# A gated cross-attention block on one core: the value table's product in 16-bit halves, its pieces staged elsewhere, and the last gate's small steps on GpSimd

## The chip, the cores and the metric

The kernel runs on one core of one Trainium2 chip. The metric is device microseconds from start to end of the program, the median of several runs; lower is better. Beside these runs there is one profiled execution, from which all rows below come. The engines are TensorE (PE; PEld is its weight load), VectorE (DVE), ScalarE (ACT), GpSimd (POOL) and SyncE (SP), which here only issues DMAs.

## The reference

Eight batches of 224 rows by 2048 columns pass through cross-attention against 750 context rows and then through a gated feed-forward block with a table of 512 slots:

```
x = x + tanh(g_xattn) * attention(layernorm(x), ctx, ctx, mask)     # 32 heads, 8 KV heads, 64 wide
h = layernorm(x)
query = h @ Wq.T                                                    # 64 wide
router = (query @ Wr.T) @ (aux_keys @ Wr.T).T / sqrt(48) + log_rel  # 512 slots, top 8 kept
w = softmax(query . aux_keys[top] / 8 + log_rel[top])
aux = (w @ aux_values[top]) @ Wvd.T @ Wvu.T                         # 512 slots -> 2048 -> 128 -> 2048
u = clip(0.5 * log1p(var) / mean(log1p(var)) + 2.5 * sigmoid(gelu(h @ Wu1.T + bu1) @ Wu2.T + bu2), 0, 5)
gate = sigmoid(gate_w1 * clip((u - 0.5) / 1.5, 0, 1) + gate_bias), 0 where < 0.05
x = x + tanh(g_ffn) * (h + gate * aux)
```

## The kernel before

There are two phases. The attention phase (to about 885 us) goes through 64 groups of seven units each; its order is written out by hand, and each engine has its own list of steps joined by semaphores. The feed-forward phase works on 14 tiles of 128 rows. The last part of the attention and the first steps of the feed-forward phase overlap.

fp32 accuracy is had from 16-bit products: a number is split in a high half (either its upper 16 bits, read in place by `high`, or a rounded copy) and a low half, the difference, and a product is summed as high x high + high x low + low x high. The attention, the wide product with Wu1 (`sum_wide`) and the last product with Wvu (`aux_part`) are done so. Two products of the feed-forward phase are fp32 instead:

- `sum_v2` (L1031 to L1038) builds the table v2 = aux_values @ Wvd.T, 512 slots by 128, once, in PSUM bank 6. The 2048 inner columns come as 8 pieces (`load_piece`: `av_stage`, 512 KB, and `wvd_stage`, 128 KB, in one of three staging slots); each piece has 8 matmuls of 128x128. Pieces 3 to 7 are loaded as slots come free (`v2_piece`). The staging slots lie in the arena behind the tiles x2b[0] to x2b[2], over xn, k_raw and k_lo of the attention. ScalarE copies v2 out (L813).
- `sum_z(t)` (L1079 to L1083) multiplies v2 with the turned weights `w_t` of tile t: four matmuls of 128x128. Ahead of it `turn_w` transposes the softmax weights and `copy_w` (ScalarE, L789) copies them out of PSUM; behind it `round_z` (L793) and `split_z` (L1409) split the result.

SyncE's queue at the border of the phases (L478 to L496) is, in this order: Wvu; a wait for the last scores; b1, w2, rel; pieces 0 to 2; the spill of the last batch's 96 lower rows, twelve DMAs, after a wait for x_added; a wait until these have landed; pieces 3 to 7; the six reloads x2b[0] to x2b[5], from the fourth on after the end of sum_v2; the stores.

TensorE's list between the phases (L1099 to L1121): turn_h, sum_query(0,0), the key products, sum_wide and sum_query of tile 0, turn_h(1,0), v2 pieces 0 and 1, quarter 2 of tile 0, turn_h(1,1), pieces 2 and 3, quarter 3 of tile 0, turn_h(1,2), pieces 4 and 5, turn_h(1,3), route(0), pieces 6 and 7. Then iterations t = 1 to 13: sum_query(t, 0 to 2), sum_wide(t, 0), turn_w(t-1), sum_query(t, 3), ..., route(t), sum_z(t-1), the rest of sum_wide, with turn_h(t+1, j) between, and from t = 8 on `aux_part` of finished tiles. `turn_h(t, j)` transposes a quarter of a normalised tile, ScalarE rounds it (`round_h`, L699), VectorE takes the low half (`split_h`, L1293).

VectorE's list of an iteration holds, among others, split_h and stage_h, `select` (the top 8 of the router row, L1362 to L1376), `dot` (L1357), `join_query` (L1388), which route(t) waits for, statistics of later tiles in iterations 1 to 5 (L1260), and `finish` (L1405), the last addition to a quarter of a tile. ScalarE does the exp of the weights (`weigh`), the GELU, and the copies.

GpSimd, after the attention, scales the keys and takes their low half (L621, L623), computes the roots of the tiles' variances (`root2`), low halves of Wvu (L633), and then the gates of the tiles in six chains of small operations (`GATES`, L659 to L671, each with a wait on the one before). The last tile's gate is computed by VectorE (L1501 to L1512) with ScalarE's exps (L842, L845) between, in the tail, where the 12 last `aux_part` of tiles 11, 12 and 13 are finished and stored.

## Time and profile before

| | |
|---|---|
| median of 3 runs (lowest, highest) | 1178.43 us (1178.39, 1180.54) |
| profiled execution: its own time | 1179.06 us |
| profiled execution: span, first to last instruction | 1177.3 us |
| granted TensorE clock, mean of the span | 0.999 |
| busy: PE, DVE, ACT, POOL | 97%, 80%, 78%, 76% |
| attention; overlap and v2; tiles 1 to 13; tail | to 885; 885 to 916; 916 to 1165; to 1177 us |

Shares of the whole span average over two phases with different lists. TensorE's matmuls are pipelined, so their modelled ends overlap the next start; the spacing of starts is the price of one. The table by stage and the timelines are therefore read beside the shares. The chain that ended last runs for 73% over TensorE and for 20% over GpSimd; the latter is in the attention.

### The profile page before, as it was taken

What the parts mean: (1) busy time and instruction counts of PE and PEld (TensorE: products, weight loads), DVE (VectorE), ACT (ScalarE), POOL (GpSimd) and SP (SyncE); (2) the same over time, 40 slices, a digit from 0 to 9 for tenths busy, and PEclk for the clock granted to TensorE, in tenths of its full rate; (3) what the DMA queues carried; (4) which work ended last, traced back from release to release, by engine and by line L of the source; (5) the groups of instructions that cost most, each with busy time, mean ns of one, the idle gap of its engine ahead of it and who ended that gap; (6) DMA issues with size and microseconds to landing.
All of it is one profiled execution on the core that took longest, in us unless ns stands there. A gap on an engine that the chain in (4) does not pass through costs nothing.

```text
span 1177.3 us, 35064 instructions
## 1 busy us (share of the span) xinstructions
PE 1139.6 (97%) x14385; PEld 913.8 (78%) x14642; DVE 944.6 (80%) x2255; ACT 916.7 (78%) x1226; POOL 889.9 (76%) x804
## 2 busy tenths in 40 slices
PE   5999999999999999999999999999999999999997
PEld 3888888888888888888888888888887665555554
DVE  5988888888888888888888888888874899676765
ACT  5899898888998898998899988999881444555544
POOL 6899999999999999999999999999991110404222
PEclk9999999999999999999999999999999999999999
DMA  9421231132114212311321131121225500011224
GB/s 336 148 69 48 57 116 45 52 83 97 42 42 116 70 48 57 115 49 48 86 93 42 46 78 49 42 58 51 62 87 182 209 2 1 1 68 77 107 99 152
DMA packets 60735, 95.09 MB, mean 81 GB/s; under 512 B 35233, under 2 KB 44449, under 8 KB 56482
## 3 DMA queue, kind: packets, MB, share of 16 engines
q1 hardware_dynamic: 59858, 91.79, 25.4%
q8 instruction: 118, 1.93, 0.7%
q10 hardware_dynamic: 720, 1.05, 0.3%
q14 instruction: 39, 0.32, 0.1%
HBM read 71.75 MB, written 20.97 MB: 79 GB/s over the span
## 4 chain that ended last, share of the span: by engine, by line
PE 73%; POOL 20%; DMA 2%; issue 2%; DVE 2%; SPq 1%; ACT 0%; DVEq 0%; POOLq 0%
POOL arena L590 14%; PE psum L985 12%; PE psum L932 12%; PE psum L909 11%; PE psum L939 6%; PE psum L920 6%; PE psum L962 5%; PE psum L956 5%; PE psum L957 5%; PE psum L1066 3%; POOL arena L557 2%; PE psum L972 2%; PE psum L999 2%; PE psum L887 2%; POOL arena L610 1%
## 5 line engine op out<-in xcount | busy, mean ns | idle before, releaser
L590 POOL TENSOR_TENSOR arena<-arena 128x768 bf16<-128x768 f32 x448 | 651.8, 1470 | 40.2 <-ACT arena L719 37.6
L1303 DVE CUSTOM_DVE_ANT_0 arena<-psum,arena 128x750 f32<-128x750 f32 x448 | 420.5, 939 | 127.4 <-PE psum L920 121.9
L719 ACT ACTIVATE arena<-psum 128x768 f32<-128x768 f32 x448 | 362.2, 809 | 89.4 <-PE psum L939 89.3
L723 ACT ACTIVATE arena<-arena,neg_max 128x750 f32<-128x750 f32 x448 | 410.9, 917 | 3.8 <-DVE neg_max L1303 3.7
L932 PE MATMUL psum<-ident,arena 128*128 128x128 f32 x1792 | 268.8, 273 | 0.0
L956 PEld LDWEIGHTS psum<-arena 128*128 128x128 bf16 (+1 forms) x2688 | 194.7, 98 | 57.6
L909 PE MATMUL psum<-arena 128*128 128x512 bf16 x674 | 222.5, 384 | 14.9 <-DVE arena L1200 0.8
L957 PE MATMUL psum<-arena 128*128 128x64 bf16 (+1 forms) x2688 | 222.2, 193 | 0.0
L956 PE MATMUL psum<-arena 128*128 128x65 bf16 (+1 forms) x2688 | 221.9, 194 | 0.0
L957 PEld LDWEIGHTS psum<-arena 128*128 128x128 bf16 (+1 forms) x2688 | 178.5, 98 | 53.2
L932 PEld LDWEIGHTS psum<-ident,arena 128*128 128x128 f32 x1792 | 206.7, 140 | 4.3
L939 PE MATMUL psum<-ident,arena 128*128 128x128 f32 x896 | 171.5, 273 | 0.2 <-ACT arena L719 0.2
L920 PE MATMUL psum<-arena 128*128 128x238 bf16 x896 | 167.5, 268 | 0.9 <-DVE neg_max L1303 0.9
L962 PE MATMUL psum<-arena 128*128 128x65 bf16 (+1 forms) x2688 | 160.1, 194 | 1.3 <-POOL arena L590 1.3
L985 PE MATMUL psum<-arena 128*128 128x512 bf16 x648 | 156.8, 384 | 1.5
L985 PEld LDWEIGHTS psum<-arena 128*128 128x128 bf16 x672 | 63.6, 96 | 75.0 <-issue 0.8
L962 PEld LDWEIGHTS psum<-arena 128*128 128x128 bf16 (+1 forms) x2688 | 114.9, 98 | 1.9 <-POOL arena L590 1.9
L939 PEld LDWEIGHTS psum<-ident,arena 128*128 128x128 f32 x896 | 112.2, 141 | 0.5 <-ACT arena L719 0.4
L699 ACT ACTIVATE arena<-psum 128x512 bf16<-128x512 f32 x56 | 33.3, 597 | 96.2 <-PE psum L972 96.2
L1246 DVE SCALAR_TENSOR_TENSOR arena<-psum,r_den,arena 128x64 f32<-128x64 f32 x448 | 97.5, 278 | 2.3
L557 POOL TENSOR_TENSOR arena<-arena 128x750 bf16<-128x750 f32 x64 | 92.1, 1439 | 1.8 <-DMA arena<-in_k_t 1.8
L909 PEld LDWEIGHTS psum<-arena 128*128 128x128 bf16 x896 | 87.8, 98 | 6.1 <-issue 0.8
(161 smaller groups left out, 1267.1 us busy)
## 6 DMA issues: line engine op xcount, KB each, us to landing
arena<-in_k_t SPq DMA_DIRECT2D x128, 187.5 KB, 3.2
arena<-in_v_rows SPq DMA_DIRECT2D x64, 192.0 KB, 2.5
out<-arena SPq DMA_DIRECT2D x12, 1024.0 KB, 3.9
arena<-in_x_top SPq DMA_DIRECT2D x8, 1024.0 KB, 5.3
arena<-in_x_rest SPq DMA_DIRECT2D x8, 768.0 KB, 4.5
spill<-arena SPq DMA_DIRECT2D x96, 64.0 KB, 2.2
arena<-spill SPq DMA_DIRECT2D x6, 1024.0 KB, 10.6
arena<-in_w_t SPq DMA_DIRECT2D x4, 1024.0 KB, 19.9
```

The source lines that it names most:

```text
L590: pool.tensor_tensor(p_lo[:, n % RING, :], p_sb[:, n % RING, :], high(p_sb[:, n % RING, :]), ALU.subtract).then_inc(p_split, 1)
L719: act.activation(p_sb[:, n % RING, :], flat_ps[:, turned_at(n):turned_at(n) + CW], ACT.Copy).then_inc(evac_a, 1)
L723: act.activation(s_sb[:, n % RING, 0:CTX], s_sb[:, n % RING, 0:CTX], ACT.Exp, bias=neg_max[:, n % 4, :], scale=-1.0).then_inc(exped, 1)
L909: pe.matmul(flat_ps[:, score_at(n) + cols.start:score_at(n) + cols.stop], q_t[:, pair % 2, half, turn, :], kk, start=(i == 0), stop=(i == 1))
L920: mm = pe.matmul(flat_ps[:, score_at(n) + cols.start:score_at(n) + cols.stop], q_t[:, g // 2 % 2, half, turn, :], kk, start=(i == 0), stop ...
L932: pe.transpose(flat_ps[:, at:at + 128], s_sb[:, n % RING, c * 128:(c + 1) * 128], ident[:, :])
L939: mm = pe.transpose(flat_ps[:, at:at + 128], s_sb[:, n % RING, c * 128:(c + 1) * 128], ident[:, :])
L956: pe.matmul(o, hi, v_hi[0:rows, u, c, :], start=(c == 0), stop=False, skip_group_check=True)
L957: pe.matmul(o[:, 0:D], hi, v_lo[0:rows, u, c, :], start=False, stop=False, skip_group_check=True)
L962: mm = pe.matmul(o, lo, v_hi[0:rows, u, c, :], start=False, stop=(c == NCH - 1), skip_group_check=True)
L985: mm = pe.matmul(psum[:, 2, :], h[:, j, kk, :], w, start=(k == 0 and n == 0), stop=(k == KC - 1 and n == 2))
L1303: dve.tensor_tensor_reduce(s_sb[:, n % RING, 0:CTX], flat_ps[:, score_at(n):score_at(n) + CTX], mask_sb[:, max(n % UNITS - REP + 1, 0), :] ...
```

## The change

- `sum_v2` computes all its products in three 16-bit parts. For each piece ScalarE rounds the Wvd part (`round_wvd`, new), and GpSimd takes the low halves of both (`split_piece`, new: two subtractions of 128x512 and one of 128x256). TensorE waits for `v2_split` instead of the DMA. Its list takes the pieces as 0 to 2, 3 and 4, 5 and 6, 7.
- The staging slots move to where k_raw, k_lo, v_raw and v_hi lie, the low halves to where xn lies. Pieces 0 and 1 are loaded after the last scores and v_split, ahead of b1, w2 and rel; piece 2 after the last value product. x2b waits for the end of sum_v2 from the third tile on.
- `sum_z(t)` from t = 5 on is done in three 16-bit parts. GpSimd rounds v2 and takes its low half once, and takes w's low half for each tile (`split_w`), ahead of the gate's chain of that tile.
- The last tile's gate is computed by GpSimd instead of VectorE; VectorE waits for it ahead of tile 13's first finish.

The diff, cut to its core (declarations of semaphores, and of the arena's views, are left out in part):

```diff
+Z_HALVED = 5
...
-        stage_at = used["ffn"] + 3 * HID
+        stage_at = keys_at
+        lo_at = xn_at
+        hi_at = lo_at + STAGE_SLOTS * (NSLOT + VB)
...
+        v2_lo = keys_raw[:, 0:2 * VB].bitcast(BF16).rearrange("p (m n) -> p m n", m=4)
+        w_lo = keys_raw[:, 2 * VB:4 * VB].bitcast(BF16).rearrange("p (m n) -> p m n", m=4)
...
             sp.dma_start(wvu, wvu_t).then_inc(wvu_loaded, 16)
+            sp.wait_ge(v_split, GROUPS)
             sp.wait_ge(scored, NU)
+            load_piece(0)
+            load_piece(1)
             sp.dma_start(b1_rows, b1).then_inc(rows_loaded, 16)
             sp.dma_start(w2_rows, w2).then_inc(rows_loaded, 16)
             sp.dma_start(rel_rows, rel).then_inc(rel_rows_loaded, 16)
-            for i in range(STAGE_SLOTS):
-                load_piece(i)
+            sp.wait_ge(valued, NU)
+            load_piece(2)
             spill_rest(BATCH - 1)
...
-                if i == 3:
+                if i == 2:
                     sp.wait_ge(v2_piece, KC // 2)
...
+            def split_piece(i):
+
+                slot = i % STAGE_SLOTS
+                pool.wait_ge(v2_loaded[slot], 32 * (1 + i // STAGE_SLOTS))
+                if i >= STAGE_SLOTS:
+                    pool.wait_ge(v2_piece, i - STAGE_SLOTS + 1)
+                for kk in range(2):
+                    pool.tensor_tensor(av_lo[:, slot, kk, :], av_stage[:, slot, kk, :], high(av_stage[:, slot, kk, :]),
+                                       ALU.subtract).then_inc(v2_split, 1)
+                pool.wait_ge(wvd_rounded, i + 1)
+                pool.tensor_tensor(wvd_lo[:, slot], wvd_stage[:, slot], wvd_hi[:, slot], ALU.subtract).then_inc(v2_split, 1)
+
+            pool.wait_ge(q_turned, 2 * PAIRS + 1)
+            split_piece(0)
+            split_piece(1)
...
             pool.tensor_tensor(keys_lo[:, :], keys_raw, keys_hi[:, :], ALU.subtract).then_inc(keys_split, 1)
+
+            for i in range(2, KC // 2):
+                split_piece(i)
+
+            def split_w(t):
+                pool.wait_ge(w_t_ready, t + 1)
+                if t > Z_HALVED:
+                    pool.wait_ge(z_summed, t)
+                pool.tensor_tensor(w_lo, w_t, high(w_t), ALU.subtract).then_inc(w_split, 1)
...
+            pool.wait_ge(v2_ready, 1)
+            pool.tensor_scalar(v2_hi, v2, 1.0, None, ALU.mult).then_inc(v2_rounded, 1)
+            pool.wait_ge(v2_rounded, 1)
+            pool.tensor_tensor(v2_lo, v2, v2_hi, ALU.subtract).then_inc(v2_halved, 1)
+            split_w(5)
             pool.wait_ge(mean_inverted, 1)
...
+            split_w(6)
...
             for tiles in GATES:
+                if tiles[0] > 0:
+                    for t in tiles:
+                        split_w(t)
...
+            small(pool.tensor_scalar(column(7), ga[:, u:u + 1], tanh_gf[:, 0:1], None, ALU.mult))
+            split_w(u)
+            pool.wait_ge(last_exped, 1)
+            small(pool.tensor_scalar(column(1), column(0), 3.0e38, 1.0, ALU.min, ALU.add))
+            small(pool.tensor_tensor(column(2), column(1), one, ALU.pow))
+            small(pool.tensor_scalar(column(1), column(2), 2.5 / (TAU_HIGH - TAU_LOW), norm_var[:, u:u + 1], ALU.mult, ALU.add))
+            pool.tensor_scalar(column(3), column(1), 0.0, 1.0, ALU.max, ALU.min).then_inc(last_clipped, 1)
+            pool.wait_ge(last_exped, 2)
+            small(pool.tensor_scalar(column(5), column(4), 3.0e38, 1.0, ALU.min, ALU.add))
+            small(pool.tensor_tensor(column(6), column(5), one, ALU.pow))
+            small(pool.tensor_scalar(column(5), column(6), EARLY_EXIT, None, ALU.is_ge))
+            small(pool.tensor_tensor(column(1), column(5), column(6), ALU.mult))
+            pool.tensor_tensor(aux_scale[:, u:u + 1], column(1), column(7), ALU.mult).then_inc(factor_ready, 1)
...
             round_h(0, 3)
+            round_wvd(0)
+            round_wvd(1)
...
             act.activation(rk_aug[0:BOT, :], psum[0:BOT, 4, :], ACT.Copy).then_inc(tables_ready, 1)
+            for i in range(2, 5):
+                round_wvd(i)
             round_h(1, 1)
+            round_wvd(5)
+            round_wvd(6)
             round_h(1, 2)
+            round_wvd(7)
...
-                    pe.wait_ge(v2_loaded[i % STAGE_SLOTS], 32 * (1 + i // STAGE_SLOTS))
+                    pe.wait_ge(v2_split, 3 * i + 3)
...
-            sum_v2(range(0, 2))
+            sum_v2(range(0, 3))
...
-            sum_v2(range(2, 4))
+            sum_v2(range(3, 5))
...
-            sum_v2(range(4, 6))
+            sum_v2(range(5, 7))
             turn_h(1, 3)
             route(0)
-            sum_v2(range(6, 8))
+            sum_v2(range(7, 8))
...
-            dve.wait_ge(last_exped, 1)
-            last(dve.tensor_scalar(column(1), column(0), 3.0e38, 1.0, ALU.min, ALU.add))
...
             split_z(TILES - 1)
-            finish(TILES, 4)
...
-            for i in range(5, 4 * len(TAIL)):
+            for i in range(4, 4 * len(TAIL)):
+                if i == 4 * (len(TAIL) - 1):
+                    dve.wait_ge(factor_ready, 1)
                 finish(TILES, i)
```

## Rows read from the trace of the kernel before

**Rows 1.** Table by stage: window, its length, busy us per engine, clock, DMA share, GB/s

```profile
884.90:915.50 30.60, 30.12 (x225) 22.96 (x228) 16.49 (x37) 5.24 (x10) 3.50 (x4) 1.00 0.59 178
1026.40:1165.00 138.60, 137.64 (x830) 78.17 (x845) 94.87 (x178) 77.29 (x97) 38.21 (x101) 1.00 0.21 84
```

**Rows 2.** The chain in order of time: start us, us, what

```profile
912.09 3.57 PE psum L1035 x32
915.66 1.34 PE psum L999 x24
925.39 0.89 PE psum L1082 x8
```

**Rows 3.** Timeline of TensorE, sum_v2: start us, us, line, operation [idle before]

```profile
891.76 3.84 PE L1035 MATMUL psum<-arena 128*128 128x128 f32 x32
901.18 2.05 PE L1035 MATMUL psum<-arena 128*128 128x128 f32 x16 [0.24 <-DMA arena<-in_wvd_t]
```

**Rows 4.** Timeline of SyncE's queue: the last spill, the load of piece 3

```profile
886.84 7.78 SPq L432 DMA_DIRECT2D spill<-arena  x12
897.88 0.43 SPq L476 DMA_DIRECT2D arena<-in_wvd_t  x1
```

**Rows 5.** GpSimd's groups by shape, whole span: count | busy us, mean ns | idle

```profile
L598 POOL TENSOR_TENSOR arena<-arena 128x384 bf16<-128x384 f32 x64 | 57.1, 893 | 0.0
L654 POOL TENSOR_TENSOR ga<-gb,minus_one 128x1 f32<-128x1 f32 x8 | 4.5, 563 | 0.7
L633 POOL TENSOR_TENSOR arena<-arena 128x512 bf16<-128x512 f32 x4 | 4.2, 1040 | 0.0
L601 POOL TENSOR_SCALAR arena<-arena,ln_scale,ln_bias 128x512 f32<-128x512 f32 x1 | 0.8, 767 | 0.0
```

**Rows 6.** Timeline of GpSimd at the end of the attention

```profile
877.92 4.70 POOL L590 TENSOR_TENSOR arena<-arena 128x768 bf16<-128x768 f32 x3 [0.40 <-ACT arena L719]
887.34 1.60 POOL L621 TENSOR_SCALAR arena<-arena 128x512 f32<-128x512 f32 x1 [4.72 <-PE psum L1103]
889.02 1.16 POOL L623 TENSOR_TENSOR keys_lo<-arena,keys_hi 128x512 bf16<-128x512 f32 x1
```

**Rows 7.** Timelines of TensorE and VectorE, from turn_h(1,3) to route(1)

```profile
910.20 0.60 PE L972 MATMUL psum<-ident,arena 128*128 128x128 f32 x4
...
923.93 1.02 PE L1092 MATMUL psum<-arena 128*128 128x512 f32 x2
...
916.09 0.69 DVE L1376 CUSTOM_DVE_ANT_0 arena<-psum,arena 128x512 f32<-128x512 f32 x1
...
922.49 0.26 DVE L1388 TENSOR_TENSOR arena<-psum,arena 64x128 f32<-64x128 f32 x1
```

**Rows 8.** Timelines of GpSimd, ScalarE and TensorE, iterations 6 and 7

```profile
1004.63 0.23 POOL L645 TENSOR_SCALAR scal_neg<-scal 128x4 f32<-128x4 f32 x1
...
1006.27 0.58 ACT L789 ACTIVATE arena<-psum 128x512 f32<-128x512 f32 x1
...
1009.32 1.05 PE L1082 MATMUL psum<-arena 128*128 128x128 f32 x8
...
1020.21 0.29 POOL L659 TENSOR_SCALAR ga<-learned,scal 128x7 f32<-128x7 f32 x1 [3.80 <-DVE learned L1357]
...
1021.70 0.59 ACT L789 ACTIVATE arena<-psum 128x512 f32<-128x512 f32 x1
...
1032.76 0.33 POOL L671 TENSOR_SCALAR aux_scale<-ga,tanh_gf 128x7 f32<-128x7 f32 x1 [0.18 <-POOL ga L670]
```

**Rows 9.** Table by stage, the tail in slices of a microsecond, columns as rows 1

```profile
1168.00:1169.00 1.00, 1.00 (x7) 0.41 (x5) 0.86 (x6) 0.00 (x0) 0.00 (x0) 1.00 1.08 442
1171.00:1172.00 1.00, 0.35 (x2) 0.00 (x0) 1.00 (x2) 0.00 (x0) 0.00 (x0) 1.00 1.05 315
1175.00:1176.00 1.00, 0.00 (x0) 0.00 (x0) 0.00 (x0) 0.00 (x0) 0.00 (x0) 0.71 0.92 354
```

**Rows 10.** Timeline of VectorE, the last finishes

```profile
1168.76 4.70 DVE L1405 SCALAR_TENSOR_TENSOR arena<-psum,aux_scale,arena 128x512 f32<-128x512 f32 x7
```

More of the change, by code:

```diff
@@ L673, in _, with column @@
             u = TILES - 1
+            one = minus_one[:, u:u + 1]
+            def column(i):
+                return last_col[:, i:i + 1]
             pool.wait_ge(weighed, TILES)
-            small(pool.tensor_tensor(ga[:, u:u + 1], wsum_all[:, u:u + 1], minus_one[:, u:u + 1], ALU.pow))
-            pool.tensor_scalar(last_col[:, 7:8], ga[:, u:u + 1], tanh_gf[:, 0:1], None, ALU.mult).then_inc(factor_ready, 1)
+            small(pool.tensor_tensor(ga[:, u:u + 1], wsum_all[:, u:u + 1], one, ALU.pow))
+            small(pool.tensor_scalar(column(7), ga[:, u:u + 1], tanh_gf[:, 0:1], None, ALU.mult))
[11 more added lines that the diff above has]
+            pool.tensor_tensor(aux_scale[:, u:u + 1], column(1), column(7), ALU.mult).then_inc(factor_ready, 1)
         @block.scalar
@@ L1031, in sum_v2 @@
                 for i in pieces:
[L1032 removed]
+                    slot = i % STAGE_SLOTS
+                    pe.wait_ge(v2_split, 3 * i + 3)
                     for kk in range(2):
+                        wide = wvd_hi[:, slot, kk, :]
                         for m in range(4):
[L1035 to L1036 removed]
+                            cols = slice(m * 128, (m + 1) * 128)
+                            values = high(av_stage[:, slot, kk, cols])
+                            pe.matmul(psum[:, 6, cols], values, wide, start=(i == 0 and kk == 0 and m == 0), stop=False, skip_group_check=True)
+                            pe.matmul(psum[:, 6, cols], values, wvd_lo[:, slot, kk, :], start=False, stop=False, skip_group_check=True)
+                            mm = pe.matmul(psum[:, 6, cols], av_lo[:, slot, kk, cols], wide, start=False,
                                            stop=(i == KC // 2 - 1 and kk == 1), skip_group_check=True)
@@ L1079, in sum_z @@
             def sum_z(t):
-                pe.wait_ge(w_t_ready, t + 1)
-                for m in range(4):
-                    mm = pe.matmul(psum[:, 6, 0:128], v2[:, m, :], w_t[:, m, :], start=(m == 0), stop=(m == 3))
+                if t < Z_HALVED:
+                    pe.wait_ge(w_t_ready, t + 1)
+                    for m in range(4):
+                        mm = pe.matmul(psum[:, 6, 0:128], v2[:, m, :], w_t[:, m, :], start=(m == 0), stop=(m == 3))
+                else:
+                    if t == Z_HALVED:
+                        pe.wait_ge(v2_halved, 1)
+                    pe.wait_ge(w_split, t - Z_HALVED + 1)
+                    for m in range(4):
+                        for n, (v, w) in enumerate(((v2_hi[:, m, :], high(w_t[:, m, :])), (v2_hi[:, m, :], w_lo[:, m, :]),
+                                                    (v2_lo[:, m, :], high(w_t[:, m, :])))):
+                            mm = pe.matmul(psum[:, 6, 0:128], v, w, start=(m == 0 and n == 0), stop=(m == 3 and n == 2))
                 mm.then_inc(z_summed, 1)
@@ L1482, in _ @@
                 finish(t, 6)
-            done = [0]
-            def last(ins):
-                done[0] += 1
-                ins.then_inc(last_step, 1)
-                dve.wait_ge(last_step, done[0])
-            def column(i):
-                return last_col[:, i:i + 1]
             preact(TILES - 1)
```

33 lines of the change are left out of this document (20 added, 13 removed).

## The prediction

> **What bounds the kernel now.** I read the busy table and the 40 slices first, then the same table by stage, then TensorE's timeline with the other engines and SyncE's queue beside it. By stage, TensorE has no room: it is busy 30.12 of 30.60 us where v2 is built, and 137.64 of 138.60 us over tiles 8 to 13 [rows 1]. Less work on TensorE shortens the kernel, unless a wait takes its place. The reader should see that GpSimd has much room in both stretches (3.50 and 38.21 us busy), so that what matters there is not its load but when its inputs come. The last ten microseconds are another matter: the DMA share is 1.08, 1.05 and 0.92 while TensorE runs dry [rows 9].
>
> **Price of the products.** From the chain: 32 passes of sum_v2's fp32 product take 3.57 us, 112 ns each; 24 passes of 128 columns in 16 bits take 1.34 us, 56 ns each; sum_z's eight passes take 0.89 us [rows 2]. An fp32 matmul is two such passes, 223 ns; its three 16-bit replacements cost 3 x 56 = 167 ns. sum_v2 has 8 pieces of 8 matmuls: 64 x 56 ns = 3.6 us less. One sum_z goes from 0.89 to 12 x 56 ns = 0.67 us: 0.22 us less.
>
> **The v2 stage: what the halves need first.** Before, sum_v2 starts on a piece when its DMA lands; it waited once, 0.24 us, for piece 3 at 901.18 [rows 3]. Now GpSimd stands between. A piece costs it two subtractions of 512 columns, the form of L633, at 1.04 us, and one of 256 columns, which has no row: the form of L598 takes 0.89 us for 384 columns, so it lies between 0.5 and 0.89, and scaled down I take 0.63 [rows 5]. With gaps that is 2.77 us a piece. ScalarE's rounding, some 0.4 us, runs beside the first two.
>
> GpSimd is done with the last p_lo at 882.6 [rows 6] and splits pieces 0 and 1 by about 890.3, after one pause for ScalarE; TensorE comes to them at 891.76 [rows 3]. Piece 2 is split after the scaling of the keys (1.60 us) and keys_lo (1.16) [rows 6]: 890.3 + 2.9 + 2.77 = 896.0. TensorE is through two pieces at 891.76 + 2.67 = 894.4 and waits 1.5 us. It ends piece 2 at 897.3, and sum_wide(0,2), sum_query(0,2) and turn_h(1,1), 3.57 us between two v2 stretches of the old timeline, at 900.9.
>
> Piece 3 decides. Its load stays on SyncE's queue behind the twelve spill DMAs of the last batch (7.78 us from 886.84) and their landing; it was issued at 897.88 [rows 4] and landed at 901.13, as the old wait shows [rows 3]. The change does not move it. It is split at 901.15 + 2.8 = 904.0, piece 4 at 906.8. TensorE waits 3.1 us, sums piece 3, waits 1.4 us, and ends piece 4 at 908.15. Then it runs through: 3.57 for sum_wide(0,3) and its neighbours, 2.67 for pieces 5 and 6 (split at 909.5 and 912.4), 0.45 for turn_h(1,3), 1.44 for route(0), 1.34 for piece 7 (split at 915.2): 917.6, against 915.66 before [rows 2]. The stage is **2.0 us longer**: 3.6 + 0.2 us saved, some 6 us of new waits. Bounds: 3.8 us shorter with every piece in time; 4 us longer with each landing or split a microsecond later.
>
> What else is moved there I cost at nothing. Pieces 0 and 1 now go out before b1, w2 and rel, piece 2 after the last value product, in the two microseconds before the spill. x2b[2] now waits for the end of sum_v2 as x2b[3] did; its statistics are due two iterations later. root2(3) comes after the last split instead of at 895, and its factor is due near 932. ScalarE's round_h(1,1) stands behind the landing of piece 4, until 903; turn_h(1,3), its reader's reader, comes at 914. Each would cost only what its cover, 10 us or more, falls short.
>
> **A second wait behind it.** What follows hangs on turn_h(1,3), not on the stage's end. Before, 5.0 us of route and v2 products lay behind it, from 910.65; now 2.8. So while the stage's end moves 2.0 us, turn_h(1,3) moves 4.2, from 910.20 to 914.4 [rows 7]. Behind it comes a chain almost without gaps: split_h(1,3), select(0) up to the neg_top of 916.09, the exp, a table load, the GELU, the dot product and, in VectorE's queue, join_query(1) at 922.49, for which route(1) waits, 923.93 before [rows 7]. join_query has 1.2 us of slack; the chain falls 2.3 us behind TensorE. **+1.1 us**; between 0 (if select is held less) and 2.3. In tiles 2 to 5 a lag of that size lies within the slack of 1.2 us.
>
> **sum_z.** Its products now wait for w_lo, 1.04 us by L633 [rows 5], behind ScalarE's copy. For tile 5: GpSimd is free at 1004.9, rounds v2 (0.8 to 1.6 us), subtracts (1.16), and splits w, whose copy ends at 1006.85: done 1008.0 to 1008.9, needed at 1009.3 [rows 8]. One tile later the copy of 1021.70 holds up the first gate's chain: it starts near 1023.4 instead of 1020.21 and ends near 1036.3 instead of 1033.1 [rows 8], 0.7 us after the first finish of tile 0 could start; VectorE has room, and nothing behind it is due at once. Later gates have an iteration. Tiles 5 to 12 are on the path: 8 x 0.22 = **-1.8 us**; a late v2_lo would cost up to 0.5 once.
>
> The row of 512 columns at L621 took 1.60 us [rows 6], that of L601 0.77 [rows 5]; the first ran beside a busy VectorE. The Trainium skill (GPSIMD Engine Reference, section 1, Specifications) says that GpSimd shares its SBUF interfaces with VectorE and contends with some of its instructions. By that rule the rounding of v2 takes the longer time and w of tile 5 is split at 1008.9, by the faster row at 1008.0; the sum is the same by both.
>
> **The tail.** VectorE loses its small operations, the last just before the seven finishes from 1168.76 [rows 10]; the chain runs on GpSimd, slower (a pow of one column 0.57 us [rows 5], the others 0.2 to 0.35, a wait after each): I estimate 1.7 and 1.9 us for its two parts, with ScalarE's exp between. aux_scale is ready about 1170.0 instead of 1168.7. Only tile 13's four parts wait for it; VectorE reaches them at 1169.6, since tile 12's no longer stand behind small operations. Its last part ends near 1172.7 instead of 1173.46. sum_z(13) waits 0.4 us for w_lo under this. But the DMA engines are full from 1168 on [rows 9], with tile 11's megabyte at their head, which comes no earlier. Of 0.75 us I count **-0.2 us**; between 0 and -0.8.
>
> **Sum.** 2.0 + 1.1 - 1.8 - 0.2 = +1.1 us. The profiled execution took 1179.06 us, 1.76 over its span and 0.6 over the median of the runs; on the median that is 1178.43 + 1.1 = 1179.5 us. About 0.2% (2.36 us) is what a measurement of this kernel can tell from no change.
>
> **Rivals.** *GpSimd keeps up.* With pieces 3 and 4 split in time the stage gains 3.8, sum_z 1.8, the tail 0.2: 1172.6 us. For it: GpSimd's idle stretch. Against it: the load of piece 3 waits for the spill as before, and no split starts before it lands. A half-way case, one wait and no lag at route(1), is 1176. Chance of both 0.12.
>
> *The clock falls* (slower). TensorE would stand 4.5 us within six microseconds round piece 3. In the trace it ran dry near 1171.4, and the granted clock was still 1.00; in the slice from 1175 it is 0.71 [rows 9]. If it falls to the half rate at piece 3, the work up to piece 6, 1.3 + 1.3 + 3.6 + 2.7 us, runs partly at 112 ns a pass instead of 56: taking 40% of it, +3.5 us, 1183.0 in all. It decides if the split of piece 3 comes so late that the two waits nearly join. The Trainium skill (TensorE: Matmul & The Clock Gate, Part 1, What's actually happening) has the clock gated to the half rate after idleness and released by sustained work. By that rule the case comes with longer waits and may stay out with those reckoned here. Chance 0.12.
>
> *The lag stays.* VectorE, full of late statistics, does not catch up, and route(2) to route(4) wait a microsecond each: 1182.5 us. Against it: 1.2 us of slack at each. Chance 0.08.
>
> *The halves are no cheaper.* At 74 ns for a pass with new weights sum_z gives nothing back and pieces 4 to 7 cost 0.45 more each: +3.6, 1183.1 us. Against it: the 24 passes of [rows 2] load weights each. Chance 0.04.
>
> **How the numbers follow.** The forecast has 0.64, own range 1177.5 to 1181.2 (the split, the lag and the tail at their bounds). Leaving out the lowest of the first rival and the highest of the slow ones gives 1176.0 to 1183.0. Faster by over 0.2% (below 1176.07): 0.12. Slower (above 1180.8): 0.12 + 0.08 + 0.04 = 0.24. Same: 0.64.
>
> **What would show it.** In the profile after: sum_v2's pieces at 1.34 us each, with TensorE waiting for GpSimd ahead of pieces 2, 3 and 4 by about 1.5, 3.1 and 1.4 us; sum_query(1,0) near 917.6; a wait of a microsecond at route(1); sum_z at 0.67 us without a wait in tiles 5 to 12; the span's end further behind the last finish than the 3.8 us of before. The forecast is wrong if piece 3 is split before 903, if the granted clock is below 1.00 between 900 and 915, or if the whole gain of the tail reaches the end.

## The result and the profile after

The changed kernel takes **1183.24 us** (median of 6 runs, 1182.65 to 1184.12) beside 1178.74 us for the kernel before, measured with it: ratio 1.0038, 95% interval 1.0027 to 1.0048, so it is slower by 0.38%, some 4.5 us. The forecast was 1179.5 us, and the time lies 0.2 us above its range. Slow executions (three of the seven of e5_filled, one of the eleven of e1_z_only) are left out of every ratio and of e5's median; e1's median is 1177.35 us without its slow one.

The profiled execution of the changed kernel took 1182.65 us with a span of 1180.8 us (before: 1179.06 and 1177.3). Its attention ended 0.76 us earlier than in the execution before, which I do not put down to the change: the start of sum_v2 lies between 891.0 and 893.5 in all profiled executions but one (895.9). So I measure what the change does **from the first pass of sum_v2**. Before: 891.76 [rows 3]. TensorE's timeline after (start us, us, line, operation [idle before <- releaser]; L1123 is sum_v2, L1083 sum_query, L1165 turn_w, L1190 route):

```profile
891.00 0.23 PE L1123 MATMUL psum<-arena 128*128 128x128 bf16 x1
895.43 0.23 PE L1123 MATMUL psum<-arena 128*128 128x128 bf16 x1 [1.57 <-POOL arena L649]
903.21 0.23 PE L1123 MATMUL psum<-arena 128*128 128x128 bf16 x1 [2.71 <-POOL arena L649]
906.01 0.29 PE L1123 MATMUL psum<-arena 128*128 128x128 bf16 x1 [0.48 <-POOL arena L649]
914.55 1.02 PE L1190 MATMUL psum<-arena 128*128 128x512 f32 x2
917.44 1.50 PE L1083 MATMUL psum<-arena 128*128 128x128 bf16 x24
922.36 0.66 PE L1165 MATMUL psum<-ident,arena 128*128 128x128 f32 x4 [0.31 <-ACT arena L855]
927.47 0.70 PE L1190 MATMUL psum<-arena 128*128 128x512 f32 x1 [0.91 <-DVE arena L1486]
```

The reader is to see two things. Ahead of pieces 2, 3 and 4 (the second, third and fourth line) TensorE stands for GpSimd's splits, as foretold. And the stretch from the end of the value stage (the 24 passes of sum_query) to route(1), which the change does not touch, has grown: 927.47 - 917.44 = 10.03 us, against 923.93 - 915.50 = 8.43 us before [rows 2, 7]. The row of before that answers to the 917.44 one is this, from the same view:

```profile
915.50 1.50 PE L999 MATMUL psum<-arena 128*128 128x128 bf16 x24
```

Where the time went, in us (the stage from the first pass of sum_v2, the last column from there to the end of the span):

| kernel | stage ends | from there to route(1) | route(1) to the end of the span | in all |
|---|---|---|---|---|
| before | 23.74 | 8.43 | 253.37 | 285.54 |
| changed | 26.44 | 10.03 | 253.33 | 289.80 |

So 2.70 us in the stage, 1.60 us behind it, and behind route(1) nothing on balance: what sum_z gains there is given back, as the experiments show, at VectorE's lateness in tile 1 (0.9 us; of it TensorE shows a wait of 0.52 us at 938.06, for preact(1), VectorE's addition of b1 to tile 1's wide product) and in the tail (0.7 us). Together 4.3 us.

VectorE and GpSimd in the tail (L1455 is the last dot product, L667 the split of the weights of tile 13, L1503 the finishes):

```profile
1167.29 1.42 DVE L1455 CUSTOM_DVE_ANT_0 arena<-arena 128x512 f32<-128x512 f32 x1
1168.64 1.40 DVE L1503 SCALAR_TENSOR_TENSOR arena<-psum,aux_scale,arena 128x512 f32<-128x512 f32 x2
1170.16 5.57 DVE L1503 SCALAR_TENSOR_TENSOR arena<-psum,aux_scale,arena 128x512 f32<-128x512 f32 x8
...
1167.12 1.04 POOL L667 TENSOR_TENSOR arena<-arena 128x512 bf16<-128x512 f32 x1 [1.45 <-issue]
```

and before, from the same view, the last dot product and the two finishes behind it:

```profile
1164.51 0.68 DVE L1357 CUSTOM_DVE_ANT_0 arena<-arena 128x512 f32<-128x512 f32 x1
1165.11 1.41 DVE L1405 SCALAR_TENSOR_TENSOR arena<-psum,aux_scale,arena 128x512 f32<-128x512 f32 x2
```

Tile 11's last finish ends at 1168.64 + 1.40 = 1170.04, and the span 10.8 us behind it; before, it ended at 1166.52 and the span 10.8 us behind. The last finish of all, in contrast, moved only from 1173.46 [rows 10] to 1175.73, 2.27 us, while the end moved 3.5 us. The end hangs on when tile 11's megabyte can go out; the small operations that left VectorE bought nothing there. The same table as [rows 9] shows the DMA engines almost idle up to 1171 and full from there to the end, where before they were full at 1168 already (window, length, busy us of TensorE, its weight loads, VectorE, ScalarE, GpSimd, granted clock, DMA share, GB/s):

```profile
1168.00:1171.00 3.00, 2.78 (x22) 1.65 (x23) 3.00 (x7) 1.10 (x4) 1.47 (x5) 1.00 0.11 44
1171.00:1175.00 4.00, 3.41 (x16) 1.26 (x14) 3.87 (x7) 0.14 (x1) 1.40 (x5) 1.00 0.99 378
1175.00:1178.00 3.00, 0.00 (x0) 0.00 (x0) 0.72 (x2) 0.00 (x0) 0.00 (x0) 0.79 1.09 317
```

### The profile page after: what moved, and what is told of

It reads as the page before. It is cut to its first block, busy times and chain, and to the rows that moved or that the text cites. A ratio compares the mean times of both kernels' runs of the same rounds, so it can differ in the third digit from the quotient of the medians.

```text
span 1180.8 us, 35578 instructions
## 1 busy us (share of the span) xinstructions
PE 1152.3 (98%) x14742; PEld 908.0 (77%) x14742; DVE 947.2 (80%) x2247; ACT 919.8 (78%) x1234; POOL 927.4 (79%) x848
## 3 DMA queue, kind: packets, MB, share of 16 engines
q10 hardware_dynamic: 720, 1.05, 0.3%
## 4 chain that ended last, share of the span: by engine, by line
PE 76%; POOL 17%; DVE 3%; DMA 1%; issue 1%; ACT 1%; SPq 1%; DVEq 0%; POOLq 0%
PE psum L993 13%; PE psum L1016 13%; POOL arena L610 12%; PE psum L1069 11%; PE psum L1023 6%; PE psum L1004 6%; PE psum L1046 6%; PE psum L1040 5%; PE psum L1041 5%; PE psum L1155 3%; PE psum L1056 2%; PE psum L1083 2%; PE psum L971 2%; POOL arena L577 2%; POOL arena L630 1%
## 5 line engine op out<-in xcount | busy, mean ns | idle before, releaser
L993 PE MATMUL psum<-arena 128*128 128x512 bf16 x896 | 272.3, 384 | 0.8 <-DVE arena L1298 0.8
L1069 PE MATMUL psum<-arena 128*128 128x512 bf16 x672 | 161.2, 384 | 0.5 <-DVE arena L1482 0.5
```

The lines of the kernel that those rows point to most:

```text
L993: pe.matmul(flat_ps[:, score_at(n) + cols.start:score_at(n) + cols.stop], q_t[:, pair % 2, half, turn, :], kk, start=(i == 0), stop=(i == 1))
L1069: mm = pe.matmul(psum[:, 2, :], h[:, j, kk, :], w, start=(k == 0 and n == 0), stop=(k == KC - 1 and n == 2))
```

## Experiments

All times are medians of 5 or more runs (e5: 4) with the kernel before beside them on the same chip (1178.7 to 1178.9 us). Differences under a microsecond between medians of different kernels are uncertain, because the attention's own length varies by as much; where such a difference matters I use distances from the first pass of sum_v2 in the profiled execution, in the table further down.

### One part of the change at a time

**e1_z_only**: the kernel before with sum_z in halves for tiles 5 to 12 and nothing else of the change.

> Only sum_z in halves, for tiles 5 to 12; v2 in fp32 with the old loads and order, the old last gate, tile 13 in fp32. Theory: route(t) comes 0.22 us earlier from tile to tile, eight times, nothing waits: 1.7 us faster than before, about 1177.0. Rival (the waits for GpSimd eat the gain, the tail cannot use it): 1178.7.

Measured 1177.44 us, ratio 0.9991 (0.9982 to 1.0000). **e2_v2_only**: the kernel before with the value table in halves, with its loads and its order.

> Only sum_v2 in halves with the new loads and order; sum_z in fp32 and the old last gate. Theory: the v2 stage costs 2.5 us, the lag behind it at turn_w(0) and route(1) 1.7 and at preact(1) 0.9, and all of it stays to the end: 5.1 us slower than before, about 1183.8. Rival (the v2 stage costs only what my sum said, 3.1, and the rest is the tail's): 1181.8.

Measured 1183.52 us, ratio 1.0046 (1.0033 to 1.0060). **e3_tail_only**: the kernel before with the last gate's steps on GpSimd.

> Only the last gate's small steps on GpSimd; all products in fp32 as before, so that GpSimd takes no low half of w beside the last dot product. Theory (the end is set by the DMAs that begin with tile 11's megabyte): the last finish comes 0.7 us earlier and the end stays: within 0.2 us of before. Rival A (the whole gain reaches the end): 0.7 us faster. Rival B (GpSimd's slower chain is what costs in the tail): 0.7 us slower.

Measured 1178.91 us, ratio 1.0003 (0.9994 to 1.0012). The three parts give -1.3, +4.7 and +0.1 us; all of the loss comes with the value table. The waits of e2 (who waits, for whom, total us, times, longest; L1098 is sum_v2, L1165 route, L1044 sum_wide, L1140 turn_w):

```profile
PE psum L1098 <- POOL arena L650: 5.2, 3, 1.9
PE psum L1165 <- DVE arena L1461: 0.9, 1, 0.9
PE psum L1044 <- DVE arena L1457: 0.5, 1, 0.5
PE psum L1140 <- ACT arena L830: 0.3, 1, 0.3
```

In e3 the last finish comes 1.05 us earlier (1172.41 for 1173.46), but the span only 0.2 us (1177.1 for 1177.3): the tail is bound by its DMAs, as foretold.

### The tail

**e4_z13_fp32**: the changed kernel with tile 13's product in fp32, so that no split runs beside the last dot product.

```
-            split_w(u)
...
-                if t < Z_HALVED:
+                if t < Z_HALVED or t == TILES - 1:
```

> The changed kernel, but sum_z of tile 13 in fp32, so that GpSimd does not subtract beside VectorE's last dot product. Theory (the dot product took 1.42 us instead of 0.68 because both engines read SBUF at once, and tile 11's store, which sets the end, stands behind it): the dot product is back at 0.7 us and the kernel 0.7 us faster than the changed one, about 1182.5. Rival (the dot product is slow for another reason, or the end does not hang on it): 1183.2.

Measured 1182.11 us, ratio 1.0028 (1.0017 to 1.0039): 1.1 us less. Its last dot product and the finishes behind it:

```profile
1166.81 0.68 DVE L1454 CUSTOM_DVE_ANT_0 arena<-arena 128x512 f32<-128x512 f32 x1
...
1167.42 1.41 DVE L1502 SCALAR_TENSOR_TENSOR arena<-psum,aux_scale,arena 128x512 f32<-128x512 f32 x2
```

The counter-test, **e9_dummy_subtract**, is the kernel before with one such split, whose result nobody reads, beside its last dot product:

```
+            pool.wait_ge(w_t_ready, TILES)
+            pool.tensor_tensor(spare.rearrange("p (m n) -> p m n", m=4), w_t, high(w_t), ALU.subtract).then_inc(small_step, 1)
```

> The kernel before, with one added subtraction of 128x512 on GpSimd once the last tile's turned weights are copied out; its result goes to a spare place and nothing waits for it. Theory (two engines reading SBUF at once slow VectorE's last dot product, and tile 11's finishes behind it set the end): the dot product takes 1.4 instead of 0.68 us and the kernel is 0.7 us slower than before, 1179.5. Rival (a subtraction beside it does no harm): 1178.8.

Measured 1179.37 us, ratio 1.0008 (1.0000 to 1.0017), 0.6 us more. Its timeline (VectorE, GpSimd), and under it the same dot product of e3, with no split beside it:

```profile
1168.69 1.36 DVE L1360 CUSTOM_DVE_ANT_0 arena<-arena 128x512 f32<-128x512 f32 x1
...
1168.46 1.04 POOL L679 TENSOR_TENSOR arena<-arena 128x512 bf16<-128x512 f32 x1 [1.40 <-ACT arena L792]
```

```profile
1164.37 0.68 DVE L1398 CUSTOM_DVE_ANT_0 arena<-arena 128x512 f32<-128x512 f32 x1
```

The dot product takes 0.68 us alone and 1.36 to 1.42 us beside a GpSimd subtraction, and tile 11's finishes stand behind it. From route(1) to the end of tile 11's last finish it is 241.83 us in e4 and 242.57 in the changed kernel, 0.74 apart; 243.26 us in e9 and 242.59 before, 0.67 apart. This is shown from both sides. What e4 gains beyond it stays open: in its profile the span ends 10.4 us behind that finish, in the profiles of the kernel before, the changed one, e1, e2, e3 and e9 10.7 to 10.8.

### The granted clock

In the profiled execution of the changed kernel it fell just behind the longest wait (table by slices, columns as in the tail's table above, the granted clock is the number behind GpSimd's busy time):

```profile
903.00:904.00 1.00, 0.79 (x12) 0.80 (x13) 0.46 (x1) 0.51 (x2) 1.00 (x2) 0.85 0.36 128
904.00:905.00 1.00, 1.00 (x12) 1.00 (x10) 1.00 (x2) 0.42 (x1) 1.00 (x2) 0.50 0.00 0
906.00:907.00 1.00, 0.99 (x10) 0.99 (x11) 0.00 (x0) 0.00 (x0) 1.00 (x2) 0.50 0.29 90
907.00:908.00 1.00, 1.00 (x18) 0.97 (x16) 0.00 (x0) 0.00 (x0) 1.00 (x2) 0.94 0.93 376
```

**e5_filled** puts 6, 12 and 5 matmuls of 512 columns, whose result nobody reads, ahead of pieces 2, 3 and 4, where TensorE waits anyway:

```
             def sum_v2(pieces):
                 for i in pieces:
                     slot = i % STAGE_SLOTS
+                    fill({2: 6, 3: 12, 4: 5}.get(i, 0))
```

> The changed kernel with 23 extra matmuls of 128x512 (0.22 us each) into a free PSUM bank, laid into TensorE's waits ahead of v2 pieces 2, 3 and 4 (6, 12 and 5); their results are not used. The profile of the changed kernel had the clock at half rate from 903.7 to 907.0. Theory: most of that lies under waits for GpSimd, so the clock at full rate gives back 0.5 us at most, and executions without the fall take as long: 1182.7 to 1183.2. Rival (the fall of the clock is the main loss that my sum lacked): 2 to 3 us faster than the changed kernel, about 1180.5.

Measured 1182.75 us, ratio 1.0034 (1.0022 to 1.0047): 0.5 us less than the changed kernel, as the theory has it, and not 2 to 3. No trace says whether the clock stayed up in the stage. But the other profiles bound what the fall is worth. Apart from the changed kernel only e13 shows it (0.50 from 905 to 907); e2 and e4, with the same stage, and seven others stay at 1.00. The two profiled executions with the fall had waited 2.71 and 2.57 us ahead of piece 3, the others 0.9 to 2.4 us. From the first pass of sum_v2 to route(1), e4 takes 35.79 us, the changed kernel with its fall 36.47. Of these 0.68 us, 0.29 lie ahead of the fall, since piece 3 began 12.21 us behind the first pass and not 11.92; the fall itself costs 0.4 us, because the wait ahead of piece 4 (0.48 us for 1.44) takes up the rest. The lag behind the stage is 10.03 us with or without it, so the clock is not its cause.

The other executions have no trace but a mean granted clock, and it says that the fall is no accident of one. In the seven kernels that load piece 3 behind the landing of the spill (the changed one, e2, e4, e6, e10, e13, e14) 21 of 46 executions have a mean of 0.997 or less, in the four that load it early (e7, e12, e15, e16) 3 of 36. In e5, with its filling, it is none of 4, and in the kernel before, e1, e3, e9 and e11, whose value table is in fp32, none of 132. In the changed kernel it doesn't sort the times: its two executions at 0.999 took 1182.67 and 1184.12 us, the one at 1.000 1183.83, the two at 0.997 1182.65 and 1183.75, so its 4.5 us are not the clock's. But in others it costs more than 0.4 us: e2's two executions at 0.996 took 1185.01 and 1185.07 us, its three others 1183.11 to 1183.52. What decides whether it falls, and where in those executions it fell, no run here shows.

### The lag behind the stage

**e6_turn_early** tests the prediction's root, turn_h(1,3), moved ahead of pieces 5 and 6:

```
+            turn_h(1, 3)
             sum_v2(range(5, 7))
-            turn_h(1, 3)
```

> The changed kernel with turn_h(1,3) ahead of v2 pieces 5 and 6 instead of behind them, in TensorE's list. Theory (the lag behind the stage comes from how late turn_h(1,3) and route(0) are): select(0) then waits for route(0) alone and starts 1.4 us earlier, the wait at route(1), 0.9 us, and those at turn_w(0) and preact(1) go: 1.4 us faster than the changed kernel, about 1181.8. Rival (the lag hangs on the GELU's table load or on the end of sum_v2): 1183.2.

Measured 1182.64 us, ratio 1.0041 (1.0028 to 1.0054): a miss. The wait at route(1) stays 0.90 us; only the 0.31 us at turn_w(0) go. Its VectorE shows something else ahead of join_query(0) (L1486, tile 0's query, of which more below): the scaling of a quarter of a tile, 0.54 us alone, took 1.40 us here, beside GpSimd's split of piece 7:

```profile
911.70 0.69 DVE L1391 TENSOR_TENSOR arena<-psum,arena 128x512 bf16<-128x512 f32 x1 [6.32 <-ACT arena L769]
912.30 1.40 DVE L1372 TENSOR_SCALAR arena<-arena,mv_all,rstd_all 128x512 f32<-128x512 f32 x1
913.63 0.27 DVE L1486 TENSOR_TENSOR arena<-psum,arena 64x128 f32<-64x128 f32 x1
```

**e7_load_early** tests the stage: pieces 3 to 7 loaded right behind the spill's issue and not behind its landing.

```
             spill_rest(BATCH - 1)
-            sp.wait_ge(spilled[(BATCH - 1) % 3], 16 * REP * NB * ((BATCH - 1) // 3 + 1))
             for i in range(STAGE_SLOTS, KC // 2):
                 sp.wait_ge(v2_piece, i - STAGE_SLOTS + 1)
                 load_piece(i)
+            sp.wait_ge(spilled[(BATCH - 1) % 3], 16 * REP * NB * ((BATCH - 1) // 3 + 1))
```

> The changed kernel with pieces 3 to 7 loaded behind the issue of the last spill instead of behind its landing. Theory (the v2 stage is set by the chain load of piece 3, split of 3, split of 4): piece 3 is issued 1.6 us earlier, and the stage and all behind it come 1.6 us earlier: about 1181.6. Rival (GpSimd's rate over all eight pieces is the bound, or the DMAs of the spill and the loads slow each other): within 0.5 us of the changed kernel.

Measured 1181.28 us, ratio 1.0025 (1.0015 to 1.0034). The stage shortens from 26.44 to 25.08 us (from 25.76 against e4, whose clock stayed up); the lag stays.

**e10_order** moves turn_h(1,2) forward too, on the theory that VectorE's list, which begins with its operand, started too late:

```
-            sum_v2(range(3, 5))
+            sum_v2(range(3, 4))
             sum_wide(0, 3)
             sum_query(0, 3)
             turn_h(1, 2)
-            sum_v2(range(5, 7))
+            sum_v2(range(4, 6))
             turn_h(1, 3)
+            sum_v2(range(6, 7))
             route(0)
```

> The changed kernel (1183.24 us) with TensorE's hand-written order of the value stage moved: turn_h(1,2) ahead of value pieces 4 and 5, turn_h(1,3) ahead of piece 6, route(0) behind piece 6. Nothing else differs. Theory A (the wait at route(1), and the one at preact(1) behind it, come from VectorE's list, which begins with the operand of turn_h(1,2) and needs 5.2 to 5.5 us from there to tile 0's MAX8; in the changed kernel that list starts 2.6 us nearer to the end of the stage than before): with turn_h(1,2) moved forward the lag of 2.6 us behind the stage goes, and the time is 1180.8 (1180.0 to 1181.5), with no wait over 0.3 us at route(1). Theory B (the lag comes from operations of VectorE and ScalarE that are slower beside GpSimd's splits, wherever the transpose stands): 1183.2 (1182.7 to 1183.7), the wait at route(1) stays at 0.9 us.

Measured 1185.04 us, ratio 1.0049 (1.0035 to 1.0063): both theories missed the time, and the first fell, for the wait at route(1) is 0.91 us. The time above theory B comes with the clock: three of the five executions have a mean clock of 0.996 and took 1185.04 to 1185.46 us, the two at 0.999 1182.81 and 1184.38. New is a wait of 1.42 us at route(0), for join_query(0). **e12_v2_mended** is e2 with this order and the early loads.

> The kernel before (1178.8 us) with the value table in halves alone (the weights' product in fp32, the old gate), with pieces 3 to 7 loaded right behind the spill instead of behind its landing, and with turn_h(1,2), turn_h(1,3) ahead of later value pieces. The value halves alone without these two moves took 1183.5. Theory A (the two moves take away the wait ahead of piece 3 in part, 1.3 to 1.9 us, and the lag of 2.6 us behind the stage): 1179.5 (1178.8 to 1180.5), so the halves of the value table come out even and no better, because the waits ahead of pieces 2 and 4 of some 1.5 us each are left. Theory B (the lag has another root): 1181.5 to 1182.5.

Measured 1182.98 us, ratio 1.0033 (1.0021 to 1.0046), 0.5 us above the range of theory B: the lag has another root. Its trace shows it. `query_lo(0)` is ScalarE's copy of one half of tile 0's query out of PSUM, and `join_query(0)` VectorE's addition of the other. ScalarE's timeline (L845 rounds a value piece, L812 is query_lo(0)) and VectorE's join_query(0):

```profile
907.15 0.58 ACT L744 ACTIVATE arena<-psum 128x512 bf16<-128x512 f32 x1
911.82 0.42 ACT L845 ACTIVATE arena<-arena 128x256 bf16<-128x256 f32 x1 [4.09 <-DMA arena<-in_wvd_t]
912.26 0.27 ACT L812 ACTIVATE arena<-psum 64x128 f32<-64x128 f32 x1
...
912.57 0.28 DVE L1462 TENSOR_TENSOR arena<-psum,arena 64x128 f32<-64x128 f32 x1 [3.66 <-ACT arena L812]
```

query_lo(0), whose input had long been there, stood in ScalarE's list behind round_wvd(7), and that waited 4.09 us for value piece 7 to land. join_query(0) waited for it, and with it the whole of tile 0's selection. The changed kernel has the same pair, less plainly, since the landing cost only 1.04 us of idle time there:

```profile
913.27 0.42 ACT L870 ACTIVATE arena<-arena 128x256 bf16<-128x256 f32 x1 [1.04 <-DMA arena<-in_wvd_t]
913.71 0.27 ACT L837 ACTIVATE arena<-psum 64x128 f32<-64x128 f32 x1
...
914.02 0.28 DVE L1486 TENSOR_TENSOR arena<-psum,arena 64x128 f32<-64x128 f32 x1 [0.62 <-ACT arena L837]
```

Before, they ran so:

```profile
907.45 0.27 ACT L767 ACTIVATE arena<-psum 64x128 f32<-64x128 f32 x1
...
908.51 0.28 DVE L1388 TENSOR_TENSOR arena<-psum,arena 64x128 f32<-64x128 f32 x1
```

That is 915.50 - 908.51 = 6.99 us ahead of the stage's end; in the changed kernel it is 917.44 - 914.02 = 3.42 us. From join_query(0) to route(1) tile 0's chain needs 13.45 us (914.02 to 927.47), and TensorE has 8.43 us of work from the stage's end: a lead of 5.02 us is needed, 3.42 us is there, and 1.60 us is the lag that the first table shows. In e10 and e12 the lead is the same 3.42 us, and the lag 10.03 and 10.02 less 8.43. It is the same because both ends start from one event, the landing of piece 7: in all three join_query(0) begins 0.75 us behind it (the rounding and query_lo(0)), and the stage ends 4.17 us behind it (the split and the products). That is why neither the early loads nor TensorE's order moved the lag.

Two kernels take the root away, each against a kernel that differs from it in ScalarE's order alone:

```
-            round_wvd(7)
             query_lo(0)
             query_hi(0)
+            round_wvd(7)
```

In e13, e15 and e16 round_wvd(7) stands one step later still, behind the copy of turn_h(1,3).

**e13_both_orders** is e10 with it, **e14_scalar_order** the changed kernel with it, **e15_v2_orders** e12 with it.

> The changed kernel (1183.24 us) with the TensorE order of e10 and, on ScalarE, the rounding of value piece 7 moved behind query_lo(0), query_hi(0) and the copy of turn_h(1,3). Theory C (the lag's root is ScalarE's list: query_lo(0) stood behind a step that waits for piece 7's landing, and tile 0's chain from join_query(0) to join_query(1) takes 13.1 us in e10, e12 and the changed kernel alike, so every us that it begins later than 5 us ahead of the stage's end is a us of lag): join_query(0) begins some 19.4 us behind the start of sum_v2 instead of 23.0, no wait over 0.3 us at route(1) nor at turn_w(0), and 2.6 us less: 1180.6 (1179.8 to 1181.2). What stays is the wait for GpSimd ahead of the last piece. Theory D (the lag has a further root, such as VectorE's operations lengthened beside GpSimd): 1182 to 1183.5, with a wait of over 0.5 us at route(1).

Measured 1181.83 us, ratio 1.0026 (1.0017 to 1.0036).

> The changed kernel (1183.24 us) with ScalarE's order alone changed: query_lo(0) and query_hi(0) ahead of the rounding of value piece 7; TensorE's order as in the changed kernel. Theory C: VectorE is free for join_query(0) only 0.6 us earlier (the step ahead of it, split_h(1,2), ends at 913.4 and join_query(0) began at 914.0), since turn_h(1,2) comes late on TensorE, so 0.6 us: 1182.6 (1182.3 to 1182.9), with 0.3 us left at route(1). Theory D: 1183.2, the wait at route(1) stays 0.9.

Measured 1182.56 us, ratio 1.0032 (1.0022 to 1.0043). The wait left at route(1) is 0.74 us and not 0.3, and the one at preact(1) 0.75 us for 0.52.

> The kernel before (1178.9 us) with the value table in halves alone, the early loads, and both orders (the kernel of e12, which took 1183.0, with ScalarE's rounding of piece 7 moved behind query_lo(0), query_hi(0) and the copy of turn_h(1,3)). Theory C: no lag behind the stage, join_query(0) some 17.6 us behind sum_v2's start, and the stage some 24.3 us long (23.7 before), since piece 7's split ends on GpSimd 22.9 us behind the start: 1179.4 (1178.8 to 1180.0). Theory D: 1181.5 to 1183.

Measured 1180.20 us, ratio 1.0014 (1.0005 to 1.0022). The waits of TensorE in e15, all from the first value piece on:

```profile
PE psum L1098 <- POOL arena L650: 5.1, 4, 1.7
```

and its ScalarE and VectorE where e12 showed 4.09 and 3.66 us:

```profile
908.50 0.27 ACT L812 ACTIVATE arena<-psum 64x128 f32<-64x128 f32 x1
...
909.58 0.27 DVE L1462 TENSOR_TENSOR arena<-psum,arena 64x128 f32<-64x128 f32 x1
```

The distances of all that bear on it (us, columns as in the first table):

| kernel | ScalarE's order | stage ends | to route(1) | to the end | in all |
|---|---|---|---|---|---|
| e2 | as changed | 25.60 | 10.03 | 254.25 | 289.88 |
| e12 | as changed | 24.64 | 10.02 | 254.19 | 288.85 |
| e15 | query_lo(0) first | 25.44 | 8.43 | 253.34 | 287.21 |
| e10 | as changed | 26.17 | 10.03 | 253.38 | 289.58 |
| e13 | query_lo(0) first | 27.94 | 8.44 | 252.43 | 288.81 |
| e14 | query_lo(0) first | 25.40 | 9.33 | 253.24 | 287.97 |

The stretch to route(1) goes back to 8.43 and 8.44 us, to a hundredth that of before, and the stretch behind it loses another 0.85 to 0.95 us, because the wait at preact(1) goes too. e14, where turn_h(1,2) still holds VectorE, loses 0.7 of the 1.60 us, about the 0.6 expected, and nothing behind route(1). Theory C stands, with this limit: in the changed kernel two things stand in a row ahead of join_query(0). TensorE comes to turn_h(1,2) 19.98 us behind the first pass (14.42 before), so VectorE gets to join_query(0) late even where query_lo(0) is there (e14; in e6 query_lo(0) began at 911.99 and the slowed scaling ended only at 913.70); and ScalarE's order holds query_lo(0). Mending TensorE's order alone (e10) takes nothing off the lag, ScalarE's alone (e14) 0.70 us, both (e13) 1.59.

What I had not expected is that the stage grew, by 0.8 us (e12 to e15) and 1.8 us (e10 to e13), and that TensorE now stands at piece 7, for GpSimd (e13):

```profile
918.18 0.23 PE L1123 MATMUL psum<-arena 128*128 128x128 bf16 x1 [2.03 <-POOL arena L649]
```

This wait is an old limit under a new name. Piece 7 is loaded when the slot of piece 4 comes free, and split after it lands. In every kernel with the new value table that has a trace of this stage, e6 excepted, its first pass comes 0.05 to 0.07 us behind the end of its split, in the changed kernel (916.09 behind 916.03), e10 and e12 too; there the work and the waits at route(0) filled the time. So the chain from piece 4 sets the end of the stage, and what made it later lies ahead of the step that differs. In e15 piece 3 landed 8.46 us behind the first pass, in e12 7.65, and the split of piece 7 ended at 24.03 and 23.23. In e13 piece 3 landed 0.15 us later than in e10; then the clock fell, and piece 7's load was issued 1.8 us later (20.50 us behind the first pass for 18.72). So e13 and e15 came out 1.2 and 0.8 us above what I expected of them, though the lag was gone; with one trace of each, how much of this is the execution's and how much the kernel's is open.

### Can anything of it pay?

**e11_z_from_1** carries sum_z's halves back to tile 1.

> The kernel before (1178.8 us) with one thing of the change alone and carried further: the weights' product in halves for tiles 1 to 12, the halves of the second value table made by GpSimd as soon as it stands, and the halves of the weights behind root2's steps in the first passes. The value stage, the gate and tile 13 are as before. Theory A (each tile in halves gives 0.16 to 0.22 us on TensorE and what GpSimd adds hides): tiles 5 to 12 alone gave 1.3 us, so twelve tiles give 1.9 to 2.7 us: 1176.5 (1176.0 to 1177.0). Theory B (GpSimd's splits come late in the first passes, where its list is fullest, and TensorE waits for them): 1177.5 to 1179.5, with a wait of over 0.3 us for GpSimd at the weights' product of tiles 1 to 4.

Measured 1177.63 us, ratio 0.9990 (0.9981 to 0.9999): a miss for theory A. From route(1) (923.31) to the end of the span it takes 252.19 us, e1 251.70, before 253.37, so four more tiles gave nothing instead of 0.9 us. But theory B's wait for GpSimd is not there either; TensorE waits for VectorE's preact (L1422):

```profile
PE psum L1014 <- DVE arena L1422: 1.6, 4, 0.7
```

In the first tiles VectorE sets the pace, and what TensorE saves there turns into that wait. **e16_mended** is e15 with e1.

> The kernel of e15 with the weights' product in halves for tiles 5 to 12 (tile 13 in fp32, the old gate). Theory C: 1.3 us under e15, as e1 was under the kernel before: 1178.1 (1177.4 to 1178.8), so at or a little under the kernel before and over e1 (1177.4). Theory D: 1180.2 to 1181.7.

Measured 1180.07 us, ratio 1.0012 (1.0003 to 1.0021): 0.1 us under e15 and not 1.3. The stage took 0.5 us more (piece 7's wait 2.12 us instead of 1.23; 0.36 us of it in the load of piece 7 itself), the rest 1.07 us less. Whether the longer wait belongs to this kernel or to the execution is open. What comes out under both kernels is the smallest version: e1, or e11, sum_z in halves alone, 0.1% under the kernel before, and at the edge of what the runs can tell.

## Why the prediction was wrong

*Price of the products*: right. In the changed kernel piece 1 starts 1.35 us behind piece 0, 24 passes of 56 ns; 1.34 us were foretold.

*The v2 stage, +2.0 us*: right in mechanism up to piece 4, and in size. The waits were to be 1.5, 3.1 and 1.4 us; e4, whose clock stayed up, has 1.57, 2.43 and 1.44, and its stage is 25.76 - 23.74 = 2.02 us longer. Piece 3 was split 12.15 us behind the first pass (903.15 - 891.00), foretold 12.2. But behind piece 4 TensorE was to run through, with piece 7 split 1.1 us before it was needed; in e4 the split of piece 7 ended 24.35 us behind the first pass and TensorE began on the piece at 24.41, so nothing was left of that room. That the size fits to 0.02 us is in part luck.

*The second wait, +1.1 us*: **this step failed**, in its root and its size. The prediction hung the chain on turn_h(1,3). In the changed kernel VectorE did not wait for that transpose at all, and moving it (e6) left 0.90 us at route(1). The root lies in what the prediction costed at nothing under "What else is moved there": there it looked at the ScalarE rounding of piece 4 ahead of round_h(1,1), and not at that of piece 7 ahead of query_lo(0), nor at how much later turn_h(1,2) comes. Both had to go before the lag went (e13, e15). It cost 1.60 us to route(1) and 0.88 us behind it (e2, 254.25 against 253.37), 2.5 us instead of 1.1. The bound of 2.3 was worked out for another mechanism. With this term at its measured size the sum gives 2.0 + 2.5 - 1.8 - 0.2 = +2.5 us. Measured against the traces, the sum fell short by 3.2 us (4.26 less 1.1): 1.4 by this step, 0.9 by the tail, 0.7 by the stage, 0.1 by sum_z.

*sum_z, -1.8 us*: right. From route(1) to the end e1 takes 251.70 us, 1.67 less than before, 0.21 us a tile; its median shows 1.3. No wait for GpSimd in tiles 5 to 12. The rounding of v2 took 1.53 us (at 1009.35), the longer of the two times weighed.

*The tail, -0.2 us*: right that the DMAs bound it and the gate's steps buy nothing (e3: 0.1 us the other way). The second term that failed is here: missing was what tile 13's split does to VectorE, +0.7 us (e4, e9), so the tail cost time where it was to give some back. The prediction had the rule for it in hand, that GpSimd and VectorE share SBUF interfaces, which it cited from the Trainium skill (GPSIMD Engine Reference, section 1, Specifications) for GpSimd's own time. It did not turn it round. The trace agrees with it in the other direction, 0.68 us to 1.42.

*The clock*: the prediction gave the rival 0.12 and +3.5 us. In the changed kernel's profile it came true in part, 3 us at half rate, at a price of 0.4 us, because it fell where GpSimd was late anyway; the granted clock below 1.00 between 900 and 915 was one of the prediction's own signs of being wrong. Without the fall the kernel is as slow, as its execution at a mean of 1.000 shows (1183.83 us). The rule weighed there, from the Trainium skill (TensorE: Matmul & The Clock Gate, Part 1, What's actually happening), has the clock gated after idleness; both falls in a trace come behind the longest waits seen, which agrees.

With all terms as measured: 2.70 (the stage, with 0.4 of the clock's fall in it) + 1.60 + 0.88 (the lag) - 1.67 (sum_z, e1) + 0.74 (the dot product's 1.42 for 0.68 us) = 4.25 us, beside the 4.26 us that the first table gives. A fit to 0.01 us is luck: the terms come from single profiled executions of different kernels, and with e4's own end of the span for the tail (1.13 us) the sum would be 4.6.

## What to carry to other kernels

When a change puts a step that waits for a DMA into an engine's list, read every instruction that stands behind it there, down to the last such step, and ask of each who waits for its result and since when its input has been ready. Here one 0.42 us rounding in front of a 0.27 us copy held up a whole tile. Two late steps can stand in front of the same operation, and taking away one shows little or nothing until the other is gone too (e10, e14, then e13). A wait that is taken away can show one that stood beside it: with the wait at route(0) gone, TensorE stood for the split of piece 7, which had set the end of the stage before. And a GpSimd operation in a gap of its own may still lengthen the VectorE operation beside it.

## What the runs showed of the hardware

- VectorE's dot product over 128x512 with both operands in SBUF took 0.68 us alone and 1.36 to 1.42 us beside a GpSimd subtraction of 128x512, in both kernels shown.
- VectorE's scaling of 128x512 in fp32 took 0.54 us alone and 1.28 us beside GpSimd's splits (904.15 in the changed kernel; 1.40 in e6); its 64x128 subtraction 0.28 and 0.82 us (914.68).
- GpSimd's split of 128x256 took 0.67 us alone and 0.85 us beside that scaling, and one of 128x512 1.04 us.
- TensorE's granted clock went to 0.50 for some 3 us behind waits of 2.71 and 2.57 us in two profiled executions and stayed at 1.00 in nine, whose waits there were 0.9 to 2.4 us.
